# Eight units of probabilities per value block in place of four, with ten probability buffers and four contexts, in a two-layer decoder kernel

## The reference

```python
x = x + L0_attn(layernorm(x))            # 16 heads, causal, linear attention with elu+1
x = x + L0_xattn(layernorm(x), ctx)      # 16 heads, softmax over 512 context rows, masked
x = x + L0_ffn(layernorm(x))             # 8 experts, the best 2 of them by a gate
x = x + L1_attn(layernorm(x))            # 16 heads, softmax, window of 128 rows back
x = x + L1_xattn(layernorm(x), ctx)      # 8 heads, softmax minus lambda*softmax, then its own FFN
x = x + L1_ffn(layernorm(x))             # ternary weights, gelu
```

## Time and profile before

| | |
|---|---|
| runs | 907.03, 903.05, 901.1 us; median 903.05 |
| profiled execution | 900.44 us, span 898.7 us, 18973 instructions |
| PE, DVE, ACT, POOL busy | 779.1, 658.8, 480.5, 340.0 us |
| granted clock of PE, mean | 0.951 of 2.4 GHz |
| value blocks | 144 (16, 64, 32 and 32 in phases 0 to 3) |

### The profile page before, as it was taken

The page is one execution under the profiler, slowest core; times in us unless marked ns, Lnnn a source line. Parts: engine busy times, 40 slices in busy tenths (PEclk is TensorE's granted clock), DMA queues, the critical chain, the costliest instruction groups (busy, mean ns, idle before and its releaser), DMA issues.

```text
span 898.7 us, 18973 instructions
## 1 busy us (share of the span) xinstructions
PE 779.1 (87%) x6136; PEld 429.9 (48%) x6202; DVE 658.8 (73%) x2253; ACT 480.5 (53%) x998; POOL 340.0 (38%) x888
## 2 busy tenths in 40 slices
PE   1678699999999889888989999999998899988854
PEld 1346334443445445546666555443445554554543
DVE  6678777888878687766977869888958787564430
ACT  3423255464656457645656665555565566655531
POOL 8884211231324443453444623222325443522422
PEclk9799799999999899989999999999999999988995
DMA  8698902121304555526375235430034654412000
GB/s 294 158 179 189 170 4 41 26 63 19 81 6 115 126 134 96 120 48 133 78 155 94 80 68 98 78 81 3 6 80 115 124 123 62 110 29 52 7 7 6
DMA packets 123810, 77.70 MB, mean 86 GB/s; under 512 B 8184, under 2 KB 122048, under 8 KB 123584
## 3 DMA queue, kind: packets, MB, share of 16 engines
q1 hardware_dynamic: 123712, 76.50, 39.5%
HBM read 41.90 MB, written 32.90 MB: 83 GB/s over the span
## 4 chain that ended last, share of the span: by engine, by line
PE 60%; DVE 16%; issue 7%; POOL 5%; ACT 5%; DMA 4%; SPq 1%; another core or an unknown queue 1%; DVEq 0%; POOLq 0%; ACTq 0%
PE ob L1303 10%; PE mb L1241 7%; PE eb L1269 6%; PE eb L1270 5%; PE side L1159 3%; PE side L1167 3%; PE side L1150 3%; DVE junk L1743 2%; DVE mx L1751 2%; PE eb L1273 2%; DMA QP<-mrow 2%; PE eb L1264 2%; PE side L1094 2%; PE ob L1294 2%; PE side L1076 2%
## 5 line engine op out<-in xcount | busy, mean ns | idle before, releaser
L1466 ACT ACTIVATE probs<-eb 128x512 f32<-128x512 f32 (+1 forms) x512 | 273.4, 568 | 201.7 <-PE eb L1270 78.5
L1743 DVE CUSTOM_DVE_ANT_0 junk<-mb,maskq_add 128x512 bf16<-128x512 f32 x256 | 168.9, 689 | 31.8 <-PE mb L1241 17.7
L1303 PE MATMUL ob<-probs,V 128*32 128x256 f32 (+1 forms) x2048 | 133.7, 379 | 2.5 <-ACT probs L1466 2.3
L1057 POOL TENSOR_SCALAR nm<-mx 128x8 bf16<-128x8 f32 x80 | 20.2, 253 | 229.8 <-DVE mx L1743 132.7
L1751 DVE TENSOR_REDUCE mx<-mb 128x1 f32<-128x512 f32 x128 | 83.3, 684 | 28.7 <-PE mb L1241 26.5
L1269 PE MATMUL eb<-maskk_add,identb 128*128 128x512 bf16 x256 | 97.6, 381 | 7.1 <-issue 3.7
L1270 PE MATMUL eb<-QP,KS 128*128 128x512 bf16 x239 | 90.8, 380 | 0.0
L1241 PE MATMUL mb<-KS,QP 128*128 128x512 bf16 x226 | 81.6, 387 | 8.3 <-DVE mx L1743 4.7
L966 POOL TENSOR_SCALAR rstd<-mv 128x2 f32<-128x2 f32 x64 | 17.1, 268 | 179.9 <-DVE mv L1529 178.5
L1303 PEld LDWEIGHTS ob<-probs,V 128*32 128x32 f32 x2048 | 55.2, 110 | 61.9 <-issue 30.1
L1343 ACT ACTIVATE hn<-X,nshift,rstd 128x128 f32<-128x128 f32 x80 | 35.0, 486 | 50.2 <-POOL nshift L973 50.1
(11 more groups left out here) (194 smaller groups left out, 1625.7 us busy)
## 6 DMA issues: line engine op xcount, KB each, us to landing
QP<-bounce SPq DMA_DIRECT2D x48, 256.0 KB, 5.6
KS<-bounce SPq DMA_DIRECT2D x32, 384.0 KB, 6.5
bounce<-scratch SPq DMA_DIRECT2D x48, 192.0 KB, 2.3
bounce<-scratch SPq DMA_DIRECT2D x64, 128.0 KB, 2.1
KS<-bounce SPq DMA_DIRECT2D x32, 192.0 KB, 4.2
bounce<-scratch SPq DMA_DIRECT2D x16, 384.0 KB, 3.2
bounce<-scratch SPq DMA_DIRECT2D x16, 256.0 KB, 2.9
bounce<-scratch SPq DMA_DIRECT2D x48, 64.0 KB, 1.7
```

The lines of the kernel that those rows point to most:

```text
L1303: ins = nc.tensor.matmul(bank[32 * j:32 * j + 32, S - n:S], v_of(core, kt, 4 * g + j), pr[:, (j % 2) * n:(j % 2 + 1) * n], start=(first_ a ...
L1466: nc.scalar.activation(probs[:, u % PROBS, 0:n], eb[:, u % 2, 0:n], ACT.Exp, scale=SCALE[core.p]).then_inc(probs_by[1], 1)
L1743: ins = V_.tensor_tensor_reduce(junk[:, e.n % 2, :], bank, maskq_add[:, t, :], 1.0, NEG_EXP, ALU.add, ALU.max, mx[slot][:, t, h:h + 1])
```

## The change

`QUAD` goes from 4 to 8: `value_sums` multiplies eight units at a time, so there are 72 value blocks. `PROBS` goes from 8 to 10, and `CTXS` from 6 to 4, which takes as many bytes away as the two buffers add. For phase 0 a new function `first_values` takes four heads (two units) at a time: first tile 0 of all four heads, then tile 1, then the product of the running sums with the queries. In the plan a value block now costs `AV_SWITCH` once and `AV_PE` for each unit, and its buffers come free one by one. Some other costs of the plan are given other values, and the tables `URGENT`, `LATER` and `AFTER` other entries.

```diff
-PROBS, QUAD, AHEAD = 8, 4, 2
+PROBS, QUAD, AHEAD = 10, 8, 2
...
-LANES, SLOTS, WIDES, OUTS, OB, QN, MROWS, CTXS = 3, 3, 2, 3, 1, 3, 4, 6
+LANES, SLOTS, WIDES, OUTS, OB, QN, MROWS, CTXS = 3, 3, 2, 3, 1, 3, 4, 4
...
-AV_PE = (1.86, 1.17, 0.96, 1.17)
+AV_PE, AV_SWITCH = (0.33, 0.245, 0.193, 0.245), 0.19
...
-STACK_LANDS, K_LANDS = (5.7, 5.7, 5.7, 5.7), 6.5
+STACK_LANDS, K_LANDS = (5.2, 7.6, 5.2, 5.5), 6.9
...
-AFTER = {(1, 0): 3, (1, 1): 2, (1, 3): 2, (1, 4): 2, (2, 2): 3}
+AFTER = {(1, 0): 3, (1, 1): 2, (1, 3): 2, (1, 4): -1, (1, 5): -3, (2, 2): 3, (2, 5): -1, (3, 7): 2}
...
-                if p == 0:
-                    for t in range(TQ):
-                        for j in heads:
...
+            def first_values(core, g, u):
...
+                for t in range(TQ):
+                    for j in range(4):
+                        at = ((j % 2) * TQ + t) * P
+                        nc.tensor.matmul(bank[32 * j:32 * j + 32, t * P:(t + 1) * P], v_of(core, t, 4 * g + j), probs[:, (u + j // 2) % PROBS, at:at + P],
+                                         start=(g == 0 and t == 0), stop=(end and t == 0), skip_group_check=True)
+                for j in range(4):
+                    ins = nc.tensor.matmul(bank[32 * j:32 * j + 32, P:2 * P], KV[core.slot][:, 4 * g + j, :], qf[core.slot][:],
+                                           start=False, stop=end, skip_group_check=True)
+                ins.then_inc(av_done, 2)
...
                 pe.wait_ge(probs_by[MADE_BY[u + QUAD - 1]], MADE[u + QUAD - 1])
+                if core.p == 0:
+                    for g in range(QUAD // 2):
+                        first_values(core, e.g * QUAD // 2 + g, u + 2 * g)
+                    return
```

More of the change, by code:

```diff
@@ L63 @@
 SHORT_PE, SHORT_BY = 0.38, 0.38
-AV_PE = (1.86, 1.17, 0.96, 1.17)
+AV_PE, AV_SWITCH = (0.33, 0.245, 0.193, 0.245), 0.19
 NM_POOL, TURN_PE, TURN_DVE, KEEP_ACT = 1.28, 0.37, 0.28, 0.59
 ROW_SP, ROW_LANDS, SPREAD_LANDS = (0, 1.65, 1.65, 2.82), 2.0, 2.0
-STACK_LANDS, K_LANDS = (5.7, 5.7, 5.7, 5.7), 6.5
+STACK_LANDS, K_LANDS = (5.2, 7.6, 5.2, 5.5), 6.9
 ACTIVE, EARLY = 4, 4
 X_LAND, W_LANDS, ROWS_LAND = (3.2, 5.6, 7.5, 17.0, 17.7, 18.4, 19.1, 19.8), 5.2, 10.5
-CTX_LAND, CTX_LANDS = (20.5, 21.2, 21.9, 22.6, 23.3, 24.0), 6.0
+CTX_LAND, CTX_LANDS = (20.5, 21.2, 21.9, 22.6), 6.0
 TERNARY = 10
@@ L104, in take_steps @@
                   ("act", "part 0", 0.71, ("values",)), ("pool", "qf", 0.3, ("values",)), ("act", "keys kept", 0.27, ("keys",)),
-                  ("pool", "k parts", 1.96, ("part 0", "keys")), ("dve", "q parts", 1.45, ("part 0", "qf")), ("pe", "kv", 1.03, ("keys kept",)),
+                  ("pool", "k parts", 1.96, ("part 0", "keys")), ("dve", "q parts", 1.9, ("part 0", "qf")), ("pe", "kv", 1.03, ("keys kept",)),
                   ("dve", "kv kept", 0.68, ("kv",)), ("sp", "spread 0", 0.95, ("part 0",)), ("sp", "spread 1", 2.25, ("q parts", "k parts"))]
@@ L140 @@
 FIRST_OF_BUFFERS = ("ctx kept", "q kept", "gating", "gates kept", "ffn 0 kept")
-URGENT = {("end", 5): 1, ("to0", 2): 2, ("to1", 6): -1, ("to2", 5): -1, ("to2", 7): 2, ("to3", 3): 1, ("to3", 4): -1, ("to3", 5): 3, ("to3", 7): 2}
-LATER = {("end", 4): -1, ("to0", 7): -3, ("to1", 1): -3, ("to2", 6): 3}
-AFTER = {(1, 0): 3, (1, 1): 2, (1, 3): 2, (1, 4): 2, (2, 2): 3}
+URGENT = {("end", 2): 3, ("end", 4): 1, ("end", 5): 1, ("end", 7): 2, ("to0", 1): -1, ("to0", 2): 2, ("to1", 1): 1, ("to1", 6): -1, ("to1", 7): 2,
+    ("to2", 5): -1, ("to2", 7): 1, ("to3", 1): 2, ("to3", 3): 1, ("to3", 4): -1, ("to3", 5): 3}
+LATER = {("end", 1): 1, ("end", 4): -1, ("to0", 7): -3, ("to1", 1): 1, ("to1", 7): -3, ("to2", 0): 3, ("to2", 5): -3, ("to2", 6): 3}
+AFTER = {(1, 0): 3, (1, 1): 2, (1, 3): 2, (1, 4): -1, (1, 5): -3, (2, 2): 3, (2, 5): -1, (3, 7): 2}
 RANK = {"turn": -1, "nm": 0, "row": -1, "chain": 0, "keep": 4.3, "chain on TensorE": 1.5, "max": 2, "exp": 2.0, "av": 4}
@@ L318, in plan @@
                 x = exp_queue[0]
-                if (x.core.p > 0) == (e == "act") and x.made <= t and (x.n < PROBS or (x.n - PROBS) // QUAD < len(av_done) and av_done[(x.n - PROBS) // QUAD] <= t):
+                if (x.core.p > 0) == (e == "act") and x.made <= t and (x.n < PROBS or x.n - PROBS < len(av_done) and av_done[x.n - PROBS] <= t):
                     found.append((RANK["exp"], 0, "exp", None, x))
@@ L446, in plan @@
                 order[e].append((t, ev))
-                free[e] = t + AV_PE[ev.core.p] - LEAVES[e]
-                av_end = t + AV_PE[ev.core.p] + SEEN
-                av_done.append(av_end)
+                us = AV_SWITCH + QUAD * AV_PE[ev.core.p]
+                free[e] = t + us - LEAVES[e]
+                av_end = t + us + SEEN
+                av_done += [av_end - (QUAD - 1 - (j | (ev.core.p == 0))) * AV_PE[ev.core.p] for j in range(QUAD)]
                 if ev.last:
@@ L1305, in values @@
-                ins.then_inc(av_done, 1)
+                n = (S, P)[kt] if p == 2 else S
+                last = 1 if p == 2 else TK - 1
+                for j in heads:
+                    ins = nc.tensor.matmul(bank[32 * j:32 * j + 32, S - n:S], v_of(core, kt, 4 * g + j), pr[:, (j % 2) * n:(j % 2 + 1) * n],
+                                           start=(first_ and kt == 0), stop=(end and kt == last), skip_group_check=True)
+                ins.then_inc(av_done, 1)
+            def first_values(core, g, u):
+                turn_ = PHASES_TO[core] - 1
+                bank = ob[:, turn_ % OB, (g % 2) * S:(g % 2 + 1) * S]
+                end = g >= GROUPS[0] - 2
+                if g == 0:
+                    pe.wait_ge(out_kept, turn_ + 1)
+                for t in range(TQ):
[7 more added lines that the diff above has]
+                ins.then_inc(av_done, 2)
```

## The result

The changed kernel takes **916.42 us**, the median of four runs from 915.33 to 921.64, against 904.14 for the kernel before: a ratio of 1.0132, 95% interval 1.0100 to 1.0163. It is 12 us slower, where 13 us faster was forecast, and it lies outside the range. The profiled execution took 915.33 us, its span is 913.6.

The account below looks back on a forecast made before the run. TensorE, busy 87% of the span, was taken as the bound. Terms -11.4 (passes and phase 0), +0.9, +0.9 (longer blocks), -2 (end) gave -11.6: 888.8 from 900.4, set at 890 us after a median correction; range 872 to 908.

Parts of the forecast that it names:

- The moved order: New costs and tables reorder cores on all engines; priced at 0, bound 12 us either way, a tenth of TensorE's idle time.
- order neutral: The main case: the saving shows and the new order costs nothing; chance 0.50, own range 882 to 899 us.
- Fewer passes: On TensorE, 134 fewer passes between narrow and full matmuls at 0.10 us each: 13.4 us saved.
- The choice of width over data type: Passes lose time by narrow against full width (13.4 us), not by float32 against bf16 (9.6 us).
- Phase 0 in fours: Four heads in turn fill phase 0's slots: 0.42 us a block of eight, 3.4 us for eight blocks, bounds 0 to 6.4.
- Longer blocks: A block holds TensorE 1.92 us instead of 1.00; costs 0.9 us at the last block and 0.9 at the start.
- The end of the order: Three steps of other sequences go behind the last block: 2 us taken as won, between 4.7 won and 4.7 lost.
- Four contexts: Two context loads leave SP's first list; 0 to 2.8 us might be won at the start, 0 taken.
- Long before their `to1`: Later contexts load behind `to3` of sequences 0 to 3, claimed to be long before their `to1` needs them.
- Taken back by waits: Rival: TensorE reaches the next `mb` bank earlier and waits for DVE, giving back 8 to 12 us: 898 to 903; chance 0.24.
- The long block starves VectorE: Rival: no new maxima issue during a block, so DVE loses 0.6 us a block: about 918 us; chance 0.14.
- The order gains too: Rival: the new order closes a tenth of TensorE's idle time and all of 14.3 us shows: 874 us; chance 0.12.

Follow-up runs that it names:

- m2: Changed kernel with its new lists, value blocks of phases 1 to 3 cut in two again: 927.48 us, 1.0226 to the kernel before.
- q1: Changed kernel with QUAD = 4, planned again for blocks of four with the changed costs and tables: 922.90 us, 1.0184 to the kernel before.
- f1: Changed kernel with only other entries in URGENT, LATER and AFTER, found by trying for lists that end earlier: 881.69 us, 0.9775 to the kernel before.
- q2: Changed kernel with before's URGENT, LATER and AFTER, planned again for blocks of eight with the changed costs: 970.46 us, 1.0705 to the kernel before.
- f2: Kernel before, blocks of four and its own costs, with table entries found by the same trying as f1: 908.43 us, 1.0037 to the kernel before.
- m4: Kernel before with only four contexts held, same lists and blocks of four: 904.12 us, 0.9989 to the kernel before.
- e4: Kernel before with its order, buffers and contexts; only phase 0 blocks take four heads in turn: 901.82 us, 0.9989 to the kernel before.
- m1: Before's lists on every engine with pairs of value blocks merged, ten buffers, four contexts, phase 0 in fours: 949.34 us, 1.0474 to the kernel before.
- m3: As m1, but phase 0 multiplies two heads at a time as before: 953.54 us, 1.0515 to the kernel before.
- e2: Changed kernel with sequence 6's end chain put ahead of those of 5 and 7 behind the last value block: 923.35 us, 1.0238 to before.
- e1: Changed kernel with the waiting maxima of phase 3, sequence 3, moved some 8 us down TensorE's list: 914.22 us, 1.0138 to the kernel before.
- h1: Kernel before with maxima of phases 1 and 3 taken over half of the columns, lists kept: 890.40 us, 0.9831 to the kernel before.
- h2: Changed kernel with maxima of phases 1 and 3 taken over half of the columns, lists kept: 901.54 us, 0.9953 to the kernel before.
- e3: Changed kernel with the list edits of both e1 and e2: 920.06 us, 1.0200 to the kernel before.
- f4: As e1, and sequence 7's context keys, their copies and halves also moved down the lists: 913.96 us, 1.0129 to the kernel before.
- f3: f1's lists with each block of phases 1 to 3 cut in two blocks of four: 897.63 us, 0.9934 to the kernel before.

## Why the prediction was wrong

**The step that failed is "The moved order".** The prediction priced it at 0, between -12 and +12, a tenth of TensorE's idle time. It cost some 20 us: by m2 against before 23.8 in medians, 20.4 by the ratio (17 to 24), and 23.2 of idle time in single profiles. The cut blocks of m2 stand at places that were not planned for them, but q1, planned for fours with the same tables and costs, is 12 to 21 us slower than before too. The bound had no row behind it, and orders differ by far more than that: eights took 881.7, 916.4, 949.3 and 970.5 us in four orders, fours 897.6 to 927.5 in five. The forecast of "order neutral" therefore had less behind it than its 0.50. Two of the signs that the prediction named for being wrong came: a last chain longer by more than 4 us, and a gap of several us in the middle.

One number could have warned of it. `plan` gives every item of its lists a time, and its last item stands at 858.9 us in the kernel before and at 875.4 in the changed one, 16.5 later; a part of that comes from the changed costs. Among the three lists of eights with the same costs, 845.9 (f1), 875.4 (changed) and 912.5 (q2) stand in the order in which they measured. It is no safe measure: f2's lists end at 842.8, 16.1 earlier than before's with the same costs, and f2 was not faster.

**Fewer passes: right** in mechanism, and near in size. With phase 0, 14.4 to 16.2 us of the value matmuls' hold on the engine went, against 16.8 forecast; TensorE's whole busy time fell by 8.2 against m4 and 9.4 against m2. Of the time it is 8.5 to 11.1 where the order is held (14.4 to 15.9 in f1's), against 9.8 for these passes, and 5 to 7 where the fours are planned anew (q1). The choice of width over data type holds too: in m4 a full bf16 matmul of 512 columns is followed by a full float32 one of 128 columns after 216 ns, as by its like, and by a 12-wide bf16 one after 309 (medians of 60 and 22).

**Phase 0 in fours: right for the engine, too high for the time.** 1.45 in place of 1.69 is 0.24 a block of four, so 0.48 for eight units against the forecast's 0.42; the rest of the way from 3.38 to 2.76 comes from the merging. What shows lies between 1 us (e4, not told from 0) and 4 (m1 against m3). The Trainium skill, "TensorE: Matmul & The Clock Gate", Part 3, says under "What overlaps and what doesn't" that loads overlap running matmuls only where the row group differs. By that sentence loads would wait here, since all use the same rows; the trace says otherwise: e4's block has 48 loads of 110 ns, 5.3 us in a row, in 1.45 us.

**Longer blocks: right** (1.86 against 1.92).

**The end of the order: wrong in sign.** -2 was taken. The stretch from the last block grew by 6.8, of which 0.9 is the longer block with its own term; the 5.9 left is beyond the bound of 4.7. The three steps were on the chain, and `end` of sequence 5 then ran in step with that of 6; that they made it longer is not shown: e2, which puts sequence 6 first, did not shorten it. The 5.9 is a part of the order's 20, not a loss beside it. And f1 has 48.2 there too (827.77 to 875.95), so the end is not what sets the changed kernel apart from f1.

**Four contexts: 0 is right in before's order (m4), and not a property of the change.** "Long before their `to1`" failed: in e1 TensorE stood for sequence 7's context from 435.7 to 441.2. Ten buffers were not tested apart; ScalarE's exponentials waited 22.6 us for value blocks before and 16.0 now, so nothing points at them.

**The rivals.** *Taken back by waits*: not borne out. TensorE's waits for maxima grew by 8 to 9 us in all, but they are 114.8 in m2 as well, which has short blocks, so they go with the order; and with VectorE relieved (h1, h2) the gap stays. *The long block starves VectorE*: it has the sign and nearly the time (918 against 916.4), for another reason. Where blocks are merged into an order made for short ones, the waits speak for it, though no edit tests it there: VectorE waits 84.0 us before the two groups of m1 shown above, 44.2 in before and 54.9 in m4. In the changed kernel h1 and h2 speak against it, and m2, which has short blocks and is slower still. *The order gains too*: 874 was its time; f1's 881.7 shows that such orders exist, but this was not one.

Two numbers of the prediction don't come out of its own terms. The lower end of the forecast's own range is 884 (900.4 - 14.3 + 1.8 - 4.7 + 1.3), not 882, and phase 0 slots of 0.09 would give 1.0 a block, not 0.8. Neither changes the outcome.

**What stays open** is which places make up the 20 us. The burst near 434 is worth at most some 4 of them by e1, e3 and f4. The end is 6.8 longer than before's, but no edit tried made it shorter. For the rest there are only sums, and no edit tests them: TensorE's longer waits for VectorE and for DMAs, VectorE's 84.1 us of waits for scores (60.1 before, 71.5 in m4, 54.4 in f1, with 10.5 of line 1766), and more DMA and SP's queue in the chain (11% against 5%, and 5% in f1; but 8% in f3, which is faster than before).

## What to carry to other kernels

Price a change of code and the change of order that comes with it as two edits, and give the second the range that other orders of the same kernel would show, not a share of the idle time. To measure the first, hold the order and change the block; to measure the second, hold the block and change the order. What the value matmuls hold TensorE for fell by 11 us in each of two orders (148.5 to 137.5, 148.0 to 136.8): this saving did not hang on the order and could be forecast. The idle time could not, where the lists were written again, and the busy time moved with the order too. If the lists come from a model of time, read first what the model itself says of the two orders.

A long wait in a list is not worth its length. Here 7.1 us gone at one place gave back 0 to 4: the next item waited for the same burst of DMA, and part of what was won was gone at the end.

## What the runs showed of the hardware

After a wait of TensorE the next work can run at the lower clock level. In the changed kernel the granted clock was 1.00 up to the 7.1 us wait, 0.61 in the stretch of the wait, and 0.50, the level of 1.2 GHz, in the 5 us behind it; there eight records of line 1096 took 1.92 us:

```profile
443.36 1.92 PE L1096 MATMUL side<-W,cT 128*128 128x128 f32 x8
```

At 421.40, with the clock at 1.00, eight of the same line had taken 1.16. In f4, without the long wait, the mean clock was 0.83 in the same stretch. At its place a wait so costs more than its own length, though the program got little of it back.
